# Layer 0's slot table: indirect DMA writes replaced by one-hot products for all four batches

## What is computed

```python
# layer 0: attention of 16 heads, then the experts, on the normed rows
x = x + jnp.tanh(g_xattn[0]) * _L0_xattn_ref(_layernorm(x, axis=-1), ctx_1024, ctx_1024, ...)
x = x + jnp.tanh(g_ffn[0]) * _L0_ffn_ref(_layernorm(x, axis=-1), ...)

def _moe_forward(hidden_states, gate_w, w_gate, w_up, w_down):   # all 2048 tokens
    logits = (x @ gate_w.T).astype(jnp.float32)
    probs = jax.nn.softmax(logits, axis=-1)
    topk_p, topk_i = jax.lax.top_k(probs, TOP_K)
    topk_p = topk_p / jnp.sum(topk_p, axis=-1, keepdims=True)
    flat_e = topk_i.reshape(-1)
    onehot = jax.nn.one_hot(flat_e, NUM_EXPERTS, dtype=jnp.int32)
    pos_all = jnp.cumsum(onehot, axis=0) - 1
    pos = jnp.take_along_axis(pos_all, flat_e[:, None], axis=1)[:, 0]
    dispatch = dispatch.at[flat_e, pos].set(x_rep, mode='drop')
    g = jax.nn.silu(jnp.einsum('ech,eih->eci', dispatch, w_gate))
    u = jnp.einsum('ech,eih->eci', dispatch, w_up)
    y = jnp.einsum('eci,ehi->ech', g * u, w_down)
    ...
    out = (y_tok * w[:, None]).reshape(T, TOPK, H).sum(axis=1)
```

## Time and profile before

| what | us |
|---|---|
| median of 3 runs (lowest, highest) | 3014.87 (3014.83, 3016.03) |
| profiled execution, its time | 3010.2 |
| span of that execution's records | 3008.5 |
| TensorE busy | 2494.1 |
| VectorE busy | 1828.6 |
| ScalarE busy | 1169.4 |
| GpSimd busy | 755.7 |
| mean granted clock of TensorE | 0.91 |

### The profile page before, as it was taken

How to read it: one execution, slowest core, us unless ns; L and a number is a source line. 1 busy time by engine, 2 the same in 40 slices (tenths; PEclk the granted TensorE clock), 3 DMA queues, 4 the chain that set the end, 5 groups by cost and what they waited for, 6 DMA issues and landing times. The chain is left out here.

```text
span 3008.5 us, 35590 instructions
## 1 busy us (share of the span) xinstructions
PE 2494.1 (83%) x12608; PEld 1340.3 (45%) x12608; DVE 1828.6 (61%) x4072; ACT 1169.4 (39%) x2095; POOL 755.7 (25%) x462
## 2 busy tenths in 40 slices
PE   6885965484787969979989979988988988997997
PEld 2331322232444534635554544554464545454554
DVE  5664743425786657367748447757636775835775
ACT  1432422121332335146635226644415553514662
POOL 1004034251000024024424114423203342401441
PEclk7997977696696979999999999999999999999998
DMA  7411000997110020124430024441023443002442
GB/s 218 136 37 16 15 15 2 299 308 258 56 63 8 12 95 1 71 75 108 113 112 1 8 89 120 109 106 56 8 86 78 112 106 98 1 22 90 114 121 76
DMA packets 112959, 257.06 MB, mean 85 GB/s; under 512 B 36198, under 2 KB 56294, under 8 KB 106762
## 3 DMA queue, kind: packets, MB, share of 16 engines
q1 hardware_dynamic: 93978, 220.26, 24.4%
q10 hardware_dynamic: 12656, 25.97, 3.5%
q0 software_dynamic: 6144, 8.48, 1.0%
HBM read 119.81 MB, written 29.69 MB: 50 GB/s over the span
## 5 line engine op out<-in xcount | busy, mean ns | idle before, releaser
L858 POOL TENSOR_SCALAR pbuf<-pbuf,recip 128x1024 f32<-128x1024 f32 x128 | 364.4, 2847 | 947.3 <-DVE recip L762 947.3
L807 ACT ACTIVATE pbuf<-ps,least 128x1024 f32<-128x1024 f32 x256 | 284.1, 1112 | 293.9 <-DVE least L755 215.3
L755 DVE CUSTOM_DVE_ANT_0 ps<-ps,mask 128x1024 f32<-128x1024 f32 x256 | 307.9, 1244 | 140.8 <-PE ps L687 139.8
L584 POOL TENSOR_SCALAR pbuf<-pbuf,recip 128x512 f32<-128x512 f32 x128 | 200.1, 1574 | 459.8 <-DVE recip L505 459.8
L687 PE MATMUL ps<-kH,qT 64*128 64x512 f32 x1024 | 266.0, 639 | 49.7 <-ACT pbuf L807 46.9
L712 PE MATMUL ps<-work,vh 128*64 128x256 f32 x2048 | 251.4, 390 | 0.0
L555 ACT ACTIVATE pbuf<-ps,least 128x512 f32<-128x512 f32 x256 | 172.5, 685 | 155.4 <-DVE least L495 155.4
L769 DVE STREAM_TRANSPOSE pbuf<-pbuf 128x2048 f32<-128x2048 f32 (+1 forms) x128 | 226.2, 1768 | 0.0
L1631 DVE TENSOR_REDUCE mh<-ps 128x3 f32<-128x1536 f32 x86 | 150.0, 1744 | 119.1 <-PE ps L1357 63.0
L1553 ACT ACTIVATE early<-ps 128x1536 f32<-128x1536 f32 x86 | 123.8, 1440 | 250.7 <-PE ps L1368 192.2
L712 PEld LDWEIGHTS ps<-work,vh 128*64 128x64 f32 x2048 | 138.2, 138 | 95.0 <-issue 36.5
(11 more groups left out here) (371 smaller groups left out, 4089.9 us busy)
## 6 DMA issues: line engine op xcount, KB each, us to landing
work<-pbuf SPq DMA_DIRECT2D x784, 96.0 KB, 2.5
work<-pbuf ACTq DMA_DIRECT2D x240, 96.0 KB, 2.9
early<-in_L_wgu SPq DMA_DIRECT2D x22, 768.0 KB
expert_rows<-zero_rows SPq DMA_DIRECT2D x16, 1024.0 KB, 11.5
yg<-expert_rows SPq DMA_DIRECT2D x16, 1024.0 KB, 6.2
early<-in_L_wd SPq DMA_DIRECT2D x22, 384.0 KB
arena<-in_L_wo SPq DMA_DIRECT2D x8, 1024.0 KB, 9.1
arena<-in_L_wff SPq DMA_DIRECT2D x4, 2048.0 KB, 9.4
```

The source lines that it names most:

```text
L584: nc.gpsimd.tensor_scalar(x, x, recip[:, n % 8:n % 8 + 1], None, mult).then_inc(probs_ready[1], 1)
L755: nc.vector.tensor_tensor_reduce(out=x, in0=x, in1=mask, scale=1.0, scalar=FMAX, op0=add, op1=ALU.min, accum_out=least[:, n % 8:n % 8 + 1])\
L807: nc.scalar.activation(to, x, ACT.Exp, bias=least[:, n % 8:n % 8 + 1], scale=-1.0, accum_out=sums[:, n % 8:n % 8 + 1]).then_inc(taken, 1)
L858: nc.gpsimd.tensor_scalar(unit(n), unit(n), recip[:, n % 8:n % 8 + 1], None, mult).then_inc(pool_divided, 1)
```

## The change

`taken_d`, `scatter`, `hand_out` and all that fed them (`place8`, `info8`, `no_token`, `k8`, `off8`, `rank_f`, `valid`, the 128x1024 passes) are gone, and so are SyncE's fill, its wait and its read of the table. Each batch now makes its part of the table as batch 3 did, with `slots` as running sum (cleared at the start, `keep_table` adds one tile at a time on VectorE). The one-hot rows of batches 0 and 1 are made by GpSimd, in two instructions for each half tile (a subtract of two inputs, then a compare with zero in place, the second waiting for the first); those of batches 2 and 3 by VectorE in one compare. The one-hot ring has four halves and not three; a maker waits (`free_onehot`) until the product that read the half was made. TensorE's table jobs stand at steps base+51, +55.45, +59.9, +64.35 for batches 0 and 1, at +48.6, +51.6, +54.6, +57.6 for batch 2, and behind everything for batch 3. VectorE's `slot` of batch b waits for the last table product of batch b-1. SyncE loads the first experts as soon as the attention is over.

```diff
-        scattered = [sem(f"scattered_{i}") for i in range(2)]
-        def scatter(b, tiles):
-            for t in tiles:
-                for k in range(TOPK):
...
-                    nc.gpsimd.indirect_dma_start(
-                        taken_d[:, :], bass.IndirectOffsetOnAxis(place8[:, b % 2, t, k:k + 1], 0), info8[:, b % 2, t, k, :], None,
-                        bounds_check=SLOTS - 1, oob_is_err=False).then_inc(scattered[group % 2], 16)
...
-    HALVES, OH = 2 * NT, 3
-    END = B - 1
+    HALVES, OH = 2 * NT, 4
+    BY_POOL = 2
...
-        for i in range(NT):
-            at["table", END, i] = base[END] + 50 + 0.1 * i
+            for i in range(NT):
+                at["table", b, i] = int(t) + (51 + 4.45 * i if b < BY_POOL else 48.6 + 3 * i if b < B - 1 else 50 + 0.1 * i)
...
+        def free_onehot(eng, b, i):
+
+            tile, h = divmod(b * HALVES + i - OH, 2)
+            if tile < 0:
+                return
+            if h:
+                eng.wait_ge(job_ready, nth["table", tile // NT, tile % NT] + 1)
+            else:
+                eng.wait_ge(onehot_used, tile + 1)
...
-                    if b == END:
-                        for half in scattered:
-                            sp.wait_ge(half, END * NT * TOPK // 2 * 16)
-                        sp.dma_start(taken[:, :, :].rearrange("p n o -> p (n o)"), taken_d.rearrange("(p n) o -> p (n o)", p=P)).then_inc(taken_in, 16)
+                    if b == B - 1:
                         sp.wait_ge(av_done, BLOCKS // 4)
...
-                def hand_out(b):
-                    yield base[b] + 53
...
+                def marks(b):
+                    for i in range(HALVES):
+                        yield base[b] + 45 + 2.2 * i
+                        if i == 0:
+                            pool.wait_ge(job_kept, nth["place", b, 0] + 1)
+                        free_onehot(pool, b, i)
+                        here, mine, every = mark(b, i)
+                        nc.gpsimd.tensor_tensor(here, every, mine, subtract).then_inc(apart, 1)
+                        pool.wait_ge(apart, b * HALVES + i + 1)
+                        nc.gpsimd.tensor_scalar(here, here, 0.0, None, ALU.is_equal).then_inc(onehot_ready, 1)
...
-                def table():
+                def table(b):
                     for t in range(NT):
-                        k = ("table", END, t)
+                        k = ("table", b, t)
                         yield at[k]
+                        if t == 0 or b < B - 1:
+                            begin(k)
                         if t == 0:
-                            begin(k)
-                            pe.wait_ge(vals_ready, 1)
+                            pe.wait_ge(vals_ready, b + 1)
                         for h in range(2):
                             i = 2 * t + h
-                            pe.wait_ge(onehot_ready, i + 1)
+                            pe.wait_ge(onehot_ready, HALVES * b + i + 1)
...
+                    if b:
+                        v.wait_ge(onehot_ready, b * HALVES)
+                        v.wait_ge(job_ready, nth["table", b - 1, NT - 1] + 1)
+                    nc.vector.scalar_tensor_tensor(out=slot[:, :, :], in0=sel[:, :, :], scalar=-AWAY, in1=by_tile(k),
+                                                   op0=mult, op1=add).then_inc(job_kept, 1)
...
-                    for half in range(2):
-                        yield t0 + 46.3 + 1.5 * half
...
-                        link(nc.vector.tensor_tensor(junk[:, some], junk[:, some], ex[:, some, :].unsqueeze(2).broadcast_to(many), mult))
-                        yield t0 + 47.3 + 1.5 * half
-                        nc.vector.tensor_reduce(w8[:, some, :], junk[:, some], AX.X, add).then_inc(placed, 1)
...
+                    for i in range(HALVES):
+                        yield max(t0 + 45.6, at["table", b, i // 2] - 2.6 + 1.3 * (i % 2)) if b < B - 1 else t0 + 46 + 0.01 * i
...
+                        free_onehot(v, b, i)
+                        here, mine, every = mark(b, i)
+                        nc.vector.tensor_tensor(here, mine, every, ALU.is_equal).then_inc(onehot_ready, 1)
...
+                def keep_table(b):
+                    for t in range(NT):
+                        k = ("table", b, t)
+                        yield at[k] + 0.3
+                        v.wait_ge(job_ready, nth[k] + 1)
...
+                        nc.vector.tensor_tensor(slots[:, :, :], slots[:, :, :], by_pair(k), add).then_inc(job_kept, 1)
```

191 lines of the change are left out of this document (57 added, 134 removed).

## The result

The changed kernel took 3000.83 us (median of 20 runs, 2997.20 to 3008.57), the kernel before beside it 3013.85 (20 runs, 3002.70 to 3021.57): a ratio of 0.9963, interval 0.9953 to 0.9974. That is faster, by 13 us where 60 were forecast, and outside the range. On two later chips the same pair gave 0.9945 (0.9927 to 0.9962) and 0.9921 (0.9896 to 0.9946). The profiled execution took 3007.01 us, its span is 3005.3.

The account below looks back on a forecast made before the run. TensorE was taken to bound the attention of layer 0 outside stalls beside the slot writes. Terms -54 - 15.8 - 5 + 9 + 4.4 - 1 = -62.4, with 2.3 more about -60: 2955 us, range 2936 to 2988.

Parts of the forecast that it names:

- (1): Attention of layer 0: two stalls beside the slot writes of two batches go, -31.4 and -22.6, together -54 us.
- more is gained: Rival, chance 0.13: VectorE's full relief, half the table products hidden, ragged steps beside the stalls gone too; -76, 2939 us.
- (2): Behind the attention: the third stall, in the last batch's layer norm, goes, -15.8 us.
- (5): Tail: batch 2's eight VectorE compares and table tiles delay the projection and the turn of the normed rows, +4.4 us.
- (6): The last batch's own table: same compares and sums with five fewer small instructions, -1 us.
- (3): VectorE in batches 0 and 1: dropped passes outweigh added sums, scans and table columns, -5 us.
- (4): TensorE gets table products; the 8 tiles of batches 0 and 1 stand amid the attention steps, +9 us.
- the 2.3: The first two table tiles of batch 2 in the exponential steps cost 2.3 us.
- GpSimd's share: GpSimd's one-hot halves: 10 us each, enough time up to 11.6, so no one waits.
- the row of 1.18 us: One GpSimd move instruction, median 0.722 us, beside VectorE's two-input passes; a hint that a half can be dearer.
- slower than before: Rival, chance 0.07: VectorE slows GpSimd's passes to h = 19 us a half, TensorE waits 116 us; 3071 us.
- wrong if: Refuting signs: a half over 12 us, searches stopping for 20 us, or VectorE's two-input passes growing longer beside GpSimd.

Follow-up runs that it names:

- writes_one_by_one: The kernel before, with each slot write waiting until the one before it had landed: 3028.36 us, ratio 1.0014.
- before_third: The kernel before, unchanged, profiled a third time: 3017.07 us beside 3014.01.
- after_third: The changed kernel, unchanged, run a third time on another chip: 2990.61 us, ratio 0.9921 against the kernel before.
- pool_thin: The changed kernel with GpSimd's passes over one expert of 32 in each half: 2951.07 us, ratio 1.0025 against the kernel before.
- before_no_writes: The kernel before without its 96 slot writes, the table of three batches left out: 2980.03 us, comparable only up to the first gather.
- all_vector: The changed kernel with every one-hot row made by VectorE: 2959.69 us, ratio 1.003; on another chip 2957.11 us, ratio 0.9797.
- pool_eighths: The changed kernel with each GpSimd pass cut in eight: 2958.41 us, ratio 1.0035; on another chip 2959.55 us, ratio 0.9818.

## Why the prediction was wrong, step by step

**The stalls (1).** Right in cause, too small in size. The slot writes do it, and writes_one_by_one shows that one at a time doesn't. Without the stalls the search is 65.9 us shorter (422.5 to 356.6), where the forecast had 54; the ragged steps around the stalls, which stood in the rival "more is gained", go too. How the writes make signals late is still not known.

**The third stall and the tail (2), (5), (6).** Right. The forecast for the time from the last search to the first gather was -15.8 + 4.4 - 1 = -12.4. Measured: -9.2 in the first pair, -15.0 between before_third and after_third (110.7 to 95.7).

**VectorE's relief and the table products (3), (4) and the 2.3.** -5 + 9 + 2.3 = +6.3 was forecast for the search. From writes_one_by_one to pool_thin it is +14.8 (356.6 to 371.4). These are kernels on two chips, and where in it the 8 us more lie, the runs don't tell apart. This error and that in the stalls, 12 us the other way, nearly cancel, which is luck.

**GpSimd's share.** The half tile was right: 3.63 + 5.36 + 0.09 for the wait between them is 9.1 us, taken as 10, under the deadline of 11.6, and TensorE's table products of batches 0 and 1 did not wait for it. The rows before gave the compare to 0.1 us. The conclusion, "so at 10 us no one waits", is **the step that failed**. It asked only whether GpSimd would be done in time for TensorE. The two texts on contention, in the paragraph on the row of 1.18 us and in the rival "slower than before", asked how much VectorE slows GpSimd, and made the price a longer h. It runs mostly the other way: GpSimd's passes kept their length (3613 to 3735 ns, 5360 to 5601; one of 4085 in after_third), and VectorE's short instructions waited for them. The argument against it, that the searches read PSUM, was true of the searches (1.71 to 1.76 us inside a pass) and missed that a search stands in one queue behind instructions that don't. The sum lacked a term of +49.8 us.

The measured terms of the search are -65.9 + 14.8 + 49.8 = -1.3, and before_third to after_third is 422.5 to 421.2. They are steps from one of four measured searches to the next, so that they add up by construction and this sum proves nothing by itself. With the tail's -15.0 that is -16.3. The spans differ by 26.2; the other 9.9 us are behind the first gather (2444.3 to 2434.4), where these times range over 2429 to 2447 in all kernels but before_no_writes, which I can't put down to the change. In the first profile of the changed kernel the search is 10 us longer than in the two later ones, and it is longer where its granted clock is lower: steps 40 to 44 take 41.8 us at 0.71 against 36.9 at 0.91 in after_third, and 60 to 64 take 31.0 at 0.67 against 22.9 at 0.95. Why the clock differed there is open.

**What would have shown it.** Of the signs named, no remote wait, the sizes of GpSimd's passes, no wait of TensorE for GpSimd's rows and the steady expert stage came true. "9 to 11 searches in each 40 us throughout, the granted clock never at 0.56" failed (7 and 5 searches, 0.58; though from 200 to 240 us, ahead of all writes, the kernel before has only 7 too), and the last of the "wrong if" is what happened. The third stretch of the earlier trace rows was the one to watch: a part that ran well before has the most to lose.

**The range** reached to 2988 and had no case for this. Slower was one mechanism at 3071, with the same two engines in it, but the wrong one waiting. The forecast's 2955 is near what variants of the change take once the holds are gone or short: 2957.11 with VectorE alone, 2959.55 in eighths, 2951.72 with both.

**Left open.** On one chip the kernel before took 2948 us, and there the eighths and the all-VectorE kernel (2958, 2960) were 0.3% slower than it, where elsewhere they are 2% faster. Their own times are the same on both chips, so it is the kernel before that differs, by 66 to 75 us, which is about what the stalls cost. That the stalls are absent there is likely and not shown: there is no profile of the kernel before from that chip, and the changed kernel itself did not run there.

## What to carry to other kernels

Work that is moved to an idle GpSimd is not free for VectorE, even when neither waits for the other's data: each copy, cast or two-input operation in SBUF that VectorE issues beside a long GpSimd pass can last nearly as long as that pass, and everything in VectorE's queue waits with it. Cut GpSimd's passes into short pieces (0.61 and 0.85 us did here) where VectorE's queue is in the critical cycle, or let VectorE do the work; and price a moved pass by what stands in the other queue beside it, not by its deadline alone. Where indirect writes hold up other engines, first limit how many may be on their way, and look at when the last one then lands.

## What the runs showed of the hardware

- A VectorE cast of 0.6 us, a copy of 0.18 us and a two-input operation of 0.16 us lasted 4.09, 2.96 and 3.48 us beside GpSimd passes of 3.6 and 5.4 us. The same GpSimd work in pieces of 0.61 and 0.85 us took the held time from 50.8 to 6.6 us.
- GpSimd's one-hot in two passes over 128x2048 takes 9.0 us where VectorE's one compare takes 2.28. Cut in eight it is 8 x (0.61 + 0.85) = 11.7 us of busy time, and still 31 us better for the kernel.
- Indirect writes, 32 in a row, one issued every 1.28 us, hold one step of the search for 22 to 33 us, in each of three profiles and in both batches that have a search beside them. Issued one at a time, every 2.87 us, they leave no such step. With at most two on their way most of it is gone (one step of 10.0 us beside them).
- Holds of two-input VectorE operations that began in the first 0.4 us of a GpSimd compare of 5.36 us ended 3.5 us after its start, while copies that began from 1.0 us on were held until 0.15 us before its end.
- The kernel before took 2948 us on one chip and 3014 to 3022 on the others, while all_vector and pool_eighths, each on that chip and on another, stayed within 0.1%.
